# Index rows of four chunks a load and one comparison over 128x2048, in a fused attention, sampling and recurrence kernel

## What is computed

```
x = x + L0(x, cond)     # RMS norm with scale and shift, 16 heads of attention, o + o @ W_out
x = x + L1(x, cond)     # sampling between two neighbouring features
x = x + L2(cond, x)     # a GRU over the 64 tokens
x = x + L3(cond, x)     # coupled oscillators, a fourth order step for each token

# L1, for one batch element; grid = cond, 512 values
ix = (grid + 1) * 0.5 * 511;  x0 = floor(ix);  w1 = ix - x0
i0 = clip(x0, 0, 511);  i1 = clip(x0 + 1, 0, 511)
out[t, n] = (1 - w1[n]) * in[t, i0[n]] + w1[n] * in[t, i1[n]]
```

## Time and profile before

| what | value |
| --- | --- |
| median of three runs | 1520.18 us (1519.2 to 1525.58) |
| the profiled execution's own time | 1517.95 us |
| its span, first to last instruction | 1515.8 us |
| mean granted TensorE clock | 0.988 |
| busy: TensorE matmul, weight load | 1456.9 us (96%), 1278.9 us (84%) |
| busy: VectorE, ScalarE, GpSimd | 1277.4 (84%), 908.0 (60%), 765.5 us (50%) |
| moved by DMA | 109.23 MB |

### The profile page before, as it was taken

The page is one execution under the profiler, slowest core; times in us unless marked ns, Lnnn a source line. Parts: engine busy times, 40 slices in busy tenths (PEclk is TensorE's granted clock), DMA queues, the critical chain, the costliest instruction groups (busy, mean ns, idle before and its releaser), DMA issues.

```text
span 1515.8 us, 94439 instructions
## 1 busy us (share of the span) xinstructions
PE 1456.9 (96%) x41966; PEld 1278.9 (84%) x41966; DVE 1277.4 (84%) x3095; ACT 908.0 (60%) x2753; POOL 765.5 (50%) x916
## 2 busy tenths in 40 slices
PE   4689999999999999999999999999999999999997
PEld 2357666766676668999999999999999999999996
DVE  6878888888888776688888888898888888888887
ACT  5466677767776653555555555555555555555553
POOL 2457776677677755443443444344344444434432
PEclk8899999999999999999999999999999999999999
DMA  7466776677777663000000000000000000000000
GB/s 271 81 141 155 155 163 156 155 166 184 170 174 174 154 145 103 8 15 16 12 15 15 15 12 15 15 12 15 15 12 15 15 15 12 15 15 12 15 15 14
DMA packets 188216, 109.23 MB, mean 72 GB/s; under 512 B 134144, under 2 KB 165056, under 8 KB 187808
## 3 DMA queue, kind: packets, MB, share of 16 engines
q1 hardware_dynamic: 187360, 102.45, 27.7%
q10 hardware_dynamic: 448, 0.74, 0.1%
HBM read 51.14 MB, written 11.67 MB: 41 GB/s over the span
## 4 chain that ended last, share of the span: by engine, by line
PE 75%; DVE 10%; ACT 4%; DMA 4%; issue 3%; POOL 3%; SPq 0%; ACTq 0%; DVEq 0%; POOLq 0%
PE psB L1455 34%; PE psA L1484 15%; PE psA L1489 8%; PE psQ L1166 7%; PE psQ L1212 5%; PE psO L1258 4%; DMA PT<-front 2%; DVE ss L821 1%; DMA first<-qn 1%; ACT front L531 1%; ACT S L531 1%; POOL front L453 1%; DVE psA L828 1%; DVE mn L848 1%; PE psO L1246 1%
## 5 line engine op out<-in xcount | busy, mean ns | idle before, releaser
L1455 PE MATMUL psB<-first,Wx 128*128 128x64 f16 x9216 | 289.7, 193 | 1.3 <-issue 1.1
L1484 PE MATMUL psA<-ts,Cp 128*128 128x64 f16 x8160 | 280.8, 193 | 6.4 <-ACT ts L1555 6.4
L1455 PE MATMUL psB<-first,Whh 128*128 128x64 f16 x9072 | 285.6, 193 | 0.7 <-POOL first L1920 0.5
L1166 PE MATMUL psQ<-Wx,front 128*128 128x512 f16 x1152 | 280.8, 392 | 4.5 <-DVE front L980 4.1
L1455 PEld LDWEIGHTS psB<-first,Wx 128*128 128x128 f16 x9216 | 277.6, 98 | 1.6 <-issue 1.5
L1455 PEld LDWEIGHTS psB<-first,Whh 128*128 128x128 f16 x9072 | 273.4, 98 | 1.1 <-POOL first L1920 0.7
L1484 PEld LDWEIGHTS psA<-ts,Cp 128*128 128x128 f16 x8160 | 256.1, 98 | 7.5 <-ACT ts L1555 7.3
L1555 ACT ACTIVATE ts<-qst 128x256 f16<-128x256 f32 x192 | 80.1, 417 | 298.4 <-DVE qst L1668 298.4
L1166 PEld LDWEIGHTS psQ<-Wx,front 128*128 128x128 f16 x1152 | 107.9, 100 | 123.8 <-issue 13.5
L1920 POOL TENSOR_TENSOR en<-rz,dn 128x256 f32<-128x256 f32 x64 | 46.7, 729 | 259.2 <-issue 256.4
L1489 PE MATMUL psA<-ts,Cp 128*128 128x64 f16 x4080 | 161.3, 193 | 0.0
(11 more groups left out here) (199 smaller groups left out, 2842.8 us busy)
## 6 DMA issues: line engine op xcount, KB each, us to landing
rows<-rows_dram SPq DMA_DIRECT2D x64, 256.0 KB, 4.5
front<-in_x SPq DMA_DIRECT2D x32, 256.0 KB, 4.5
XR<-in_x_turned SPq DMA_DIRECT2D x32, 256.0 KB, 4.9
out<-ob SPq DMA_DIRECT2D x63, 128.0 KB, 1.7
x<-x SPq DMA_DIRECT2D x29, 224.0 KB
Whh<-in_W_qkv SPq DMA_DIRECT2D x12, 256.0 KB, 8.5
room<-in_W_hh SPq DMA_DIRECT2D x12, 256.0 KB, 2.8
room<-in_W_ih SPq DMA_DIRECT2D x12, 256.0 KB, 2.8
```

Of the source, the lines that this page charges most:

```text
L1166: last = mm(psQ[:, n, :], xn[p.u][:, i, c, :], Wqkv[:, j, c, n * D:(n + 1) * D], start=(c == 0 and t == 0), stop=(c == KC - 1 and t == 2))
L1455: last = mm(o, W_[:, i, c, g * PART:(g + 1) * PART], src[:, j, c, :], start=False, stop=False, skip_group_check=True)
L1484: mm(psF[:, s % 2, m, :], Cp[:, i, c, m * PART:(m + 1) * PART], ts_[:, 0, c, :], start=(c == 0 and m == 0 and i == 0), stop=False, skip_gr ...
```

## The change

The rows of all four chunks, i0 - 128 c for c = 0 to 3, are computed, stored and loaded, and all are compared with the same number p. A load is 128 partitions x 2048 values, 512 KB, in runs of 4 KB a partition where runs of 2 KB were. One comparison of 128x2048 builds E. `lidx` shrinks to one column, the two buffers `rows` double, and `grid_rows` has four small instructions of 64x512 where it had two. The order on every engine and in SP's queue, and all waits, stay.

```
-    lidx, gqk = sb("lidx", [PART, 2]), sb("gqk", [PART, 1])
+    lidx, gqk = sb("lidx", [PART, 1]), sb("gqk", [PART, 1])
-    rows = [sb(f"rows{u}", [PART, 2, D], F16) for u in range(2)]
+    rows = [sb(f"rows{u}", [PART, KC, D], F16) for u in range(2)]
-        nc.gpsimd.iota(lidx[:, :], pattern=[[2 * PART, 2]], base=0, channel_multiplier=1,
+        nc.gpsimd.iota(lidx[:, :], pattern=[[0, 1]], base=0, channel_multiplier=1,
...
-            for k in range(2):
-                e = v.tensor_scalar(E_of(p, b)[:, 2 * k:2 * k + 2, :].rearrange("p c n -> p (c n)"), rows[b][:, :, :].rearrange("p c n -> p (c n)"),
-                                    lidx[:, k:k + 1], None, ALU.is_equal)
-            e.then_inc(e_built, 1)
+            v.tensor_scalar(E_of(p, b).rearrange("p c n -> p (c n)"), rows[b][:, :, :].rearrange("p c n -> p (c n)"),
+                            lidx[:, 0:1], None, ALU.is_equal).then_inc(e_built, 1)
...
-            for c in range(2):
+            for c in range(KC):
                 last = v.tensor_scalar(i0h[:, c, :], i0, 1.0, float(-c * PART), ALU.mult, ALU.add)
...
-    rows = nc.dram_tensor("rows_dram", (B, 2, D), F16, kind="Internal").ap()
+    rows = nc.dram_tensor("rows_dram", (B, KC, D), F16, kind="Internal").ap()
```

## The result

The changed kernel took 1529.80 us in the median (six runs, 1526.33 to 1533.31). The kernel before, run beside it, took 1520.55 (1516.14 to 1525.58). The ratio is 1.0053, with a 95% interval of 1.0035 to 1.0071: slower by 9.3 us in the medians. The interval leaves out no change, and holds the prediction's bound of half a per cent. The profiled execution has a span of 1527.6 us, 11.8 more than before's.

A forecast was written before the change was run, and what follows sets the result against it. Bound by TensorE's chain (floor 16.45 of 16.85 us a slot), else by a loop through VectorE and GpSimd. Terms -0.5 + 1.5 + 0.3 + 4.8 = +6.1 on 1517.95 gave 1524.1, forecast as a 1526 us median; range 1514 to 1545.

The forecast's parts named there:

- The likeliest case: Whole kernel: small stall at x1 or none, 1526 us in the median, own range 1516 to 1532; chance 0.52.
- Slots of 16.9 to 17.1 us: Sign in the attention and sampling loop that the forecast is right; a slot took 16.85 us before.
- loads landing some 1 us later: Sign in SP's queue that the forecast is right: row loads landing later than the 4.5 us before.
- The build: VectorE's comparison making E: 0.78 us in place of 0.87 where undisturbed, -0.5 us in all, ends 0 and -9.8.
- the cover: VectorE's 0.31 us idle before ScalarE's squares: freeing VectorE 0.89 us earlier beside modA gains nothing by itself.
- GpSimd's hold: Longer comparison delays modA and so the end of L460 and ms: +0.1 us in 15 slots, +1.5 in all.
- The rival of a shorter GpSimd chain: One hold falls where GpSimd waits anyway, ms ends earlier, loads stay hidden: -6.8 us, 1513.4; chance 0.12.
- Grid rows: Startup: two more small operations computing index rows, once: +0.3 us, ends 0 and 2.56.
- The loads: 512 KB row loads in SP's queue delay x1, samples wait: 0.2 us in 24 slots, +4.8, ends 0 and +29.
- The first rival: x1 late in every slot, loads at the mean rate with engine gaps staying: +20.5 us, 1540.7; chance 0.32.
- the prediction's estimate from this table: Row loads: 2.8 us for the added 512 KB, x1 delayed 2.35, net stall 1.5 a slot, +37 in all.
- The transposes at 0: q/k transposes behind x1 in the queue lose nothing up to a delay of 1.4 us; far end 0.66 a slot.

The follow-up runs named there:

- e2: Kernel before with its 256 KB loads, but one 128x2048 comparison, chunks 2 and 3 being constant zeros: 1523.52 us, ratio 0.9993.
- e1: Changed kernel with its 512 KB loads, but two comparisons of 128x1024 as before: 1529.64 us, ratio 1.0035.
- e3: Changed kernel with the 256 KB load of the turned x issued behind x1's moves: 1526.55 us, ratio 1.0016.
- e5: Kernel before plus two spare 256 KB loads a slot, read by nobody, both behind x1's moves: 1530.72 us, ratio 1.0033.
- e7: Changed kernel with the second 512 KB row load issued behind x1's moves: 1529.06 us, ratio 1.0026.
- e6: Kernel before with the load of the turned x issued behind x1's moves: 1522.21 us, ratio 0.9973.
- e10: Kernel before with both loads of the next x (tokens and turned) issued behind x1's moves: 1526.64 us, ratio 1.0003.
- e11: Kernel before with the turned-x load behind x1's moves, measured again on another chip: 1527.24 us, ratio 1.0002.
- e9: Changed kernel, each 512 KB load kept as one but in runs of 2 KB by a gap in the buffer: 1531.97 us, ratio 1.0041.
- e8: Changed kernel with each 512 KB load issued as two loads of 256 KB: 1544.20 us, ratio 1.0106.
- e4: Kernel before plus two spare 256 KB loads a slot, read by nobody, ahead of x1's moves: 1562.49 us, ratio 1.0221 without the slowest run.

## Why the prediction was right, and where its steps were off

The likeliest case came in. The median lies 3.8 us above the 1526 forecast, in the range of 1514 to 1545, and just past the bound of 0.5%, which by its interval can't be told from just under it; the repeat, at 0.37%, fell on the other side. The chain of reasons held: the comparison neither gains nor loses what can be seen, and the loads cost a few microseconds in which the samples wait for x1. Slots of 16.9 to 17.1 us were named as a sign and are 17.2 in the mean (430.1 / 25); loads landing some 1 us later land 1.2 later. That the sum came so near is in part luck: it had no term for the pauses, which grew by as much as the waits of the samples, and the waits for the transposes happened to shrink. The steps:

- **The build.** 0.78 us was predicted, 0.74 to 0.75 measured; the price of width was right. Its hidden gain stayed hidden, as the cover (VectorE idle before the sums of squares) said: in the groups by line the builds' busy time fell from 74.1 us for 56 builds to 41.8 for 55, or by 0.56 us a build, while the idle time before the sums of squares grew by 22.7 us, and no time came of it. The -0.5 us taken for the undisturbed builds is not seen either.
- **GpSimd's hold.** +0.1 us in 15 slots was predicted. modA grew by 0.26 and modB shrank by 0.06, both as said, and the median slot went from 16.76 to 16.86 us (16.84 in e2), some 2 us in all. In the profiles sign, path and size were right. The waits for oT grew by more, 3.1 us here and 3.5 in e2; a sum of waits is not the loop's length. e2's time doesn't confirm the loss: its interval ends at +1.1 us. The rival of a shorter GpSimd chain falls by the slots, of which none is left near 16.6.
- **Grid rows.** 0 to 2.56 predicted, 0.3 taken; nothing is seen in the first projection's start, which scatters by more than that.
- **The loads.** The sum was near, +4.8 as 0.2 in each of 24 slots against 5.3 us by the ratio in e1 (2.7 to 7.9), but it was made up otherwise. Most slots lose nothing at x1; four to seven lose up to 1.1 us each (3.5 and 4.1 us in all), and the rest is pauses, of which the term knew nothing. The engines were used better (0.97 and 313 GB/s over 5 us) than at the mean rate of the earlier trace rows, as the chosen 0.2 supposed. The first rival, x1 late in every slot, is out by the same rows. The Trainium skill, DMA: Bandwidth & Descriptors, section Bandwidth, lists 0.95 us for 64 KB and 6.15 us for 1 MB, and the prediction's estimate from this table was +37 us in all. The measured +9.3 disagrees with that estimate. It does not disagree with the table's rate for 1 MB, 341 GB/s, beside the 335 of the stretch from 400 to 402 us; the likely fault of the estimate is to charge the added bytes at the slope between two single transfers, as if no other load ran beside them.
- **The transposes at 0.** In the changed kernel this held: 4.2 and 1.2 us of waits against 5.5. But the room for it was small. With a load put between x1 and the transposes, as in e3, e5 and e7, they waited 7.9 to 8.4 us, and in the three runs of the kernel before with its own loads moved there (e6, e10, e11) 5.8, 7.7 and 9.6. This is the step that fails when one tries to mend the change.
- **The pauses.** The prediction had no term for them, and they are as large as the samples' waits. They fall within a group, as this timeline of TensorE in the changed kernel shows:

```profile
247.73 2.46 PE L1256 MATMUL psO<-oT,Wo 128*128 128x128 f16 x41 [0.23 <-DVE oT L889]
251.10 0.56 PE L1256 MATMUL psO<-oT,Wo 128*128 128x128 f16 x7 [0.90 <-issue]
...
262.70 0.24 PE L1244 MATMUL psO<-PT,Vt 64*32 64x64 f16 x8
264.47 0.47 PE L1244 MATMUL psO<-PT,Vt 64*32 64x64 f16 x40 [1.53 <-issue]
```

After 41 of the 48 matmuls of a projection TensorE stands 0.90 us; 13 us later 1.53 us after 8 of 48. The code has no wait inside either group, so their operands are there. Over all profiles the pauses inside a group go with what stands ahead of x1: 0.9 to 1.4 us in the kernel before and e2; 4.8 to 4.9 in the changed kernel and its repeat, 6.3 in e1, 8.3 in e9, 4.8 in e8, 4.3 in e4; 0.3 to 2.2 in the six profiles with a load moved behind x1 or the spares there. They come at places that recur. In all profiles but those of e4 and e8 one pause of 0.3 to 2.4 us ends between 105 and 109 us, before the last 2 of the 48 matmuls of L1244 (L1246 before); the repeat of the changed kernel pauses before the last 26 matmuls of a group at 386.48 as the first did at 384.39, and e1 before the last 7 of a projection at 250.48 as here at 251.10. A guess is that TensorE's instructions, which the page shows as transfers of their own ("q8 instruction", 329 packets, 5.39 MB), arrive late when much stands in the queues. The recurring places fit it. Plain traffic isn't enough: e5 moves the bytes of e4 behind x1 and pauses 2.2 us. No run tested the guess, and it stays open; so does why e8's second load costs more than its bytes in a single one.

## What to carry to other kernels

One operation saved on an engine that then waits for another was worth nothing here, and its price was paid where its data comes from. Before a transfer is lengthened, look at what stands behind it in the same queue and who needs that soonest; if bytes must be added there, add them to a transfer that exists rather than as a further one, and expect a move behind the needed one to delay the next needed one instead. A gain of 0.3% on one chip should be measured again on another before it is believed.

## What was not expected of the hardware

- The same spare loads of 256 KB cost 1.4% in the fastest run (2.2% in the ratio, part of it at a lower clock) ahead of a small transfer that TensorE waits for, and 0.33% behind it.
- The same bytes cost 0.37 to 0.53% as one load of 512 KB and 1.06% as two of 256 KB; a run of 4 KB is one packet, and halving the runs cost nothing that can be seen (0.41%).
- TensorE pauses, by up to 2.9 us, inside groups of matmuls where the profile finds nothing missing, partly at the same places from run to run, and for longer in all (4.3 to 8.3 us against 0.3 to 2.2) when more stands ahead of x1 in SP's queue.
- A VectorE comparison of 0.75 us stretches a GpSimd operation that starts beside it from 1.23 to 1.49 us where two of half the width stood before, and the next one takes 1.05 us in place of 1.11.
